# A first-layer chunk moved ahead of the last tile's transposes, and the last transfers shared out anew

## What is computed

```python
e = jnp.stack([tbl_0[ids[:, 0]], ..., tbl_26[ids[:, 26]]], axis=1)      # 27 rows of 128 per sample
interactions = jnp.einsum('bfd,bgd->bfg', e, e)                         # 27 x 27 products per sample
z = jnp.concatenate([bottom, interactions[lower triangle]], axis=1)     # 128 + 351
h = jnp.concatenate([z, bottom], axis=1)                                # 607
h = jnp.maximum(h @ W_top1 + b_top1, 0.0)                               # 607 -> 512
h = jnp.maximum(h @ W_top2 + b_top2, 0.0)                               # 512 -> 256
y = h @ W_top3                                                          # 256 -> 1
```

## Time and profile before

| | |
|---|---|
| median of three runs | 378.94 us (378.78 to 379.65) |
| the profiled execution | 377.31 us |
| its span, first to last instruction | 375.5 us |
| PE busy | 338.1 us (90%) |
| POOL busy | 267.5 us (71%) |
| DVE busy | 247.9 us (66%) |
| ACT busy | 145.9 us (39%) |

### The profile page before, as it was taken

How to read it: one execution, slowest core, us unless ns; L and a number is a source line. 1 busy time by engine, 2 the same in 40 slices (tenths; PEclk the granted TensorE clock), 3 DMA queues, 4 the chain that set the end, 5 groups by cost and what they waited for, 6 DMA issues and landing times.

```text
span 375.5 us, 10311 instructions
## 1 busy us (share of the span) xinstructions
PE 338.1 (90%) x4321; PEld 326.6 (87%) x4321; DVE 247.9 (66%) x332; ACT 145.9 (39%) x280; POOL 267.5 (71%) x292
## 2 busy tenths in 40 slices
PE   0567869998999999999999989998999989997996
PEld 0456759997999999999999989998999989997985
DVE  2699997993699466953698176944598276952051
ACT  1466765615222443155313532145313522155202
POOL 6777777777777777777777777777777777775710
PEclk9998999999999999999999999999999999999999
DMA  7998874336443643345343643355243533323310
GB/s 153 232 223 242 261 209 131 86 81 163 149 121 77 193 114 89 84 100 194 78 108 68 192 108 91 83 136 166 61 111 73 192 107 96 81 60 82 63 16 1
DMA packets 47058, 45.76 MB, mean 122 GB/s; under 512 B 33033, under 2 KB 35930, under 8 KB 47013
## 3 DMA queue, kind: packets, MB, share of 16 engines
q1 hardware_dynamic: 36050, 26.88, 27.3%
q0 software_dynamic: 9184, 17.93, 18.2%
q10 hardware_dynamic: 1779, 0.30, 0.4%
HBM read 39.52 MB, written 5.55 MB: 120 GB/s over the span
## 4 chain that ended last, share of the span: by engine, by line
PE 77%; DMA 7%; DVE 6%; POOL 3%; issue 3%; ACT 3%; SPq 1%
PE work L465 41%; PE gram L492 10%; PE work L477 6%; PE work L518 4%; PE work L519 4%; PE work L520 4%; DMA raw_lo<-in_tbl 4%; DVE onehot L625 3%; DMA emb<-in_tbl,ids_all 3%; POOL emb L433 3%; PE work L535 2%; PE work L537 2%; PE work L536 2%; DVE tab_lo L610 2%; SPq L355 1%
## 5 line engine op out<-in xcount | busy, mean ns | idle before, releaser
L433 POOL DMA_INDIRECT emb<-in_tbl,ids_all x272 | 258.3, 950 | 84.0 <-issue 78.0
L625 DVE TENSOR_TENSOR onehot<-ids_bc,row_idf 125x1024 fp32r<-125x1024 int32 (+2 forms) x232 | 198.8, 920 | 35.7 <-PE work L465 29.4
L465 PE MATMUL work<-onehot,tab_hi 125*128 125x256 f32 x672 | 168.8, 291 | 24.1 <-ACT tab_hi L734 13.7
L465 PE MATMUL work<-onehot,tab_lo 125*128 125x256 f32 x672 | 165.2, 286 | 0.0
L465 PEld LDWEIGHTS work<-onehot,tab_hi 125*128 125x128 f32 x672 | 130.5, 194 | 30.0 <-issue 14.4
L465 PEld LDWEIGHTS work<-onehot,tab_lo 125*128 125x128 f32 x672 | 130.8, 195 | 0.0
L776 ACT COPY embT<-work 128x512 f32<-128x512 f32 (+1 forms) x36 | 26.9, 799 | 103.4 <-PE work L465 103.4
L492 PE MATMUL gram<-embT 128*54 128x52 f32 x1920 | 51.6, 214 | 2.3 <-ACT embT L595 2.1
L492 PEld LDWEIGHTS gram<-embT 128*54 128x54 f32 x1920 | 49.6, 130 | 4.6 <-ACT embT L595 1.3
L477 PE MATMUL work<-ident,emb 128*128 128x128 f32 x272 | 35.4, 275 | 4.7 <-DMA emb<-in_tbl,ids_all 4.7
L783 ACT COPY inter<-gram 118x416 f32<-118x416 f32 x64 | 32.4, 508 | 16.6 <-PE gram L492 14.6
(11 more groups left out here) (55 smaller groups left out, 225.5 us busy)
## 6 DMA issues: line engine op xcount, KB each, us to landing
ids_bc<-in_sel_ids SPq DMA_DIRECT2D x14, 512.0 KB, 4.4
grams<-inter SPq DMA_DIRECT2D x62, 84.5 KB
emb<-in_tbl,ids_all POOLq DMA_INDIRECT x272
ids_bc<-in_sel_ids SPq DMA_DIRECT2D x11, 256.0 KB, 9.5
misc<-in_tbl SPq DMA_DIRECT2D x3, 448.0 KB
inter<-in_tbl SPq DMA_DIRECT2D x3, 448.0 KB
raw_w<-in_W_top SPq DMA_DIRECT2D x4, 256.0 KB, 7.2
misc<-in_bottom SPq DMA_DIRECT2D x8, 128.0 KB
```

The lines of the kernel that those rows point to most:

```text
L433: pool.indirect_dma_start(out=emb[:, t % TILE_SLOTS, f, :], out_offset=None, in_=gather_tables[f], in_offset=bass.IndirectOffsetOnAxis(ap= ...
L465: mm = nc.tensor.matmul(out, part[0:k, CHUNK_AT[f] + c, :], onehot[0:k, at % RING, i * HALF:(i + 1) * HALF], start=(c == 0 and i % 2 == 0 ...
L625: nc.vector.tensor_tensor(onehot[0:k, at % RING, 0:width], ids_bc[0:k, four[0]:four[-1] + 1, :].rearrange("p i n -> p (i n)"), row_idf[0:k ...
```

## The change

It has three parts. First, the bottom chunk of half 6's first layer (12 matmuls) is moved on PE: from behind the products of tile 15 to a place ahead of its transposes. The two banks of that layer are thus claimed earlier, so three banks are left for the five groups of transposes: g3 takes the bank of g0, and g4 that of g1. Second, `take_gram` now notes the banks' uses by selections and transposes alone, since the first layer's two banks are still open when the products start. Third, the 28 packs of the last tile are shared 11, 11, 6 by SP, ACT and POOL, where it was 12, 12, 4.

```diff
-    POOL_PACKS = PACKS[5::6]
+    POOL_PACKS = PACKS[2::5]
     SP_PACKS, ACT_PACKS = [[pack for pack in PACKS if pack not in POOL_PACKS][n::2] for n in range(2)]
...
-    use, fill, used, upto = {}, {}, [0] * BANKS, {}
-
-    def claim(*key):
-        n = use["next"] = use.get("next", -1) + 1
+    use, fill, used, upto, embedded = {}, {}, [0] * BANKS, {}, [0] * BANKS
+
+    def claim(*key, n=None):
+        if n is None:
+            n = use["next"] = use.get("next", -1) + 1
         use[key] = (n % BANKS, used[n % BANKS])
         used[n % BANKS] += 1
+        if key[0] in ("select", "rows"):
+            embedded[n % BANKS] = used[n % BANKS]
...
     def take_gram(t):
-        upto["gram", t] = list(used)
+        upto["gram", t] = list(embedded)
...
-        take_rows(2 * h + 1)
+        if h + 1 == HALVES:
+            claim_mlp1(h - 1)
+            take_rows(2 * h + 1, range(BANKS - 2))
+            first = use["next"] - (BANKS - 3)
+            for g in range(BANKS - 2, NGR):
+                claim("rows", 2 * h + 1, g, n=first + g - (BANKS - 2))
+                signal("rows", 2 * h + 1, g)
+            use["next"] = first + BANKS - 1
+        else:
+            take_rows(2 * h + 1)
         take_gram(2 * h + 1)
         if h < HALVES - 1:
             take_mlp(h - 1, "mlp1")
-    take_mlp(HALVES - 2, "mlp1")
+    signal_mlp1(HALVES - 2)
...
                 mlp3(h - 2)
+                if h == HALVES - 1:
+                    mlp1(h - 1, X_ORDER[:1])
                 rows(2 * h + 1, range(NGR))
                 if h < HALVES - 1:
                     mlp1(h - 1)
                 products(2 * h + 1, range(GRAMS))
 
-            mlp1(HALVES - 2)
+            mlp1(HALVES - 2, X_ORDER[1:])
             mlp1(HALVES - 1, X_ORDER[:1])
```

## The result

The changed kernel took 375.94 us (median of 8 runs, 375.29 to 376.30). Beside it, the kernel before took 378.67 us (8 runs, 377.35 to 379.65). The ratio is 0.9933, with a 95% interval of 0.9914 to 0.9952, so 1.8 to 3.3 us less. I had forecast 377.7 us, in a range of 377.0 to 379.1.

The account below looks back on a forecast made before the run. POOL's gathers, then PE from g4's transposes on, were taken to bound the end. Moving 1.44 us into PE's idle time, less 0.2 for the banks, gains 1.24: 378.94 - 1.24 = 377.7 us, range 377.0 to 379.1.

Parts of the forecast that it names:

- Where PE has room: On PE between transposes of g3 and g4: 1.25 us idle, waiting for g4's gathers, into which the bottom chunk fits.
- The banks' wait: At tile 15's transposes: g3 waits for ACT's copy of g0, g4 for DVE's of g1; g4 starts at 346.0 to 346.15.
- The loss behind it: From g4's transposes on: 0.2 us later, bounds 0 and 0.47, passed into everything behind; products start at 347.8.
- my upper bound: Sum on PE behind the products: at most 1.44 us gained, all twelve moved matmuls without loss; forecast 1.24, lower bound 0.97.
- The packs: Tile 15's packs for half 7: all land in time, tightest by 0.6 us; new shares worth nothing, adding 0.4 us slack.
- The sign I gave: In the changed profile at the end: a rounding released by a DMA would show the prediction wrong.
- The packs didn't set the end: Rival at half 7: packs come just in time and the end moves 0.2 us later, 379.1 us; chance 0.12.
- what the three banks' hand-overs cost: Rival at tile 15's transposes: bank hand-overs of 0.35 us or more cut the gain to 0.5 to 0.97; chance 0.15.
- POOL issued six packs in 4.06 us: Rival at POOL's six packs: GpSimd stands still during DVE's ReLU of half 6, giving 380.5 us; chance 0.06.
- The looser counts: `take_gram` drops a wait for DVE's copy in each half: at most 0.2 us in the whole program, taken as 0.
- The span: Length of the profiled execution: 375.5 us before, less 1.24, gives 374.3.
- The total: Median of runs: 1.63 us above the profiled execution, carried over; 378.94 - 1.24 = 377.7 us.

Follow-up runs that it names:

- the move alone: Against the changed kernel, the bottom chunk still moved but the old pack shares 12, 12, 4 restored: 376.58 us, ratio 0.9946.
- the first set: 30 runs of the unchanged kernel before, on the chip shared by the first four experiments: 378.28 us (377.38 to 380.23).
- the chunk twice: Against the move alone, half 6's bottom chunk runs ahead of the last transposes and once more behind the products, old shares: 378.32 us, ratio 0.999.
- The chunk left out: Against the kernel before, its order and shares kept, half 6's bottom chunk isn't computed at all: 376.50 us, runs in two groups.

## Why the prediction was wrong

- **Where PE has room: right.** The wait for g4's gathers is gone, and the chunk fits there.
- **The banks' wait: right.** ACT ended the copy of g0 at 345.58 (345.04 + 0.54 in the changed trace), forecast 345.57 to 345.67; DVE that of g1 at 345.93, forecast 345.92 to 346.02. ACT began its copy of g4 at 346.74, 0.15 later than 346.59, where I had taken 0.2 for the loss.
- **The loss behind it: mis-sized.** It didn't reach the products. The piece called issue between ACT's copy and the products took 0.20 us instead of 0.35, so they started at 347.60, not 347.8, and the gain on PE was my upper bound, 1.44 instead of 1.24. (From POOL's last gather, 0.07 earlier in the changed profile, it is 1.37.) The shorter hand-over is no accident of one execution: it took 0.35 in all seven profiles with the waits of before, and 0.19 to 0.20 in all five with the chunk moved ahead of the transposes. All five also have the looser counts of `take_gram`, so which of the two shortens it stays open.
- **The packs: right.** All came in time; chunk 0's were ready on DVE 0.6 us before PE wanted them, as forecast. The new shares are worth nothing that can be measured (1.0008 alone). The sign I gave was badly chosen, though: a rounding released by a DMA was to mean that I was wrong, and chunk 0's was, without cost, since DVE asks for it earlier than PE.
- **The rivals: none came.** The packs didn't set the end; what the three banks' hand-overs cost, 0.15 at ACT's copy, didn't reach the products; POOL issued six packs in 4.06 us, in part beside DVE's ReLU.
- **The looser counts** weren't tried alone. I took 0 for them; the products of tile 15 start at 347.60 in both profiles, but the 0.15 of the hand-over may be theirs.
- **The span: right.** 374.1, forecast 374.3. That the two spans can be compared so directly is in part luck: POOL's last gather ended at nearly the same moment in both (343.81 and 343.74), and in the move alone a microsecond later.
- **The total: wrong, and this is the step that failed:** "The median of the runs lies 1.63 above the profiled one; I carry the difference over". I took that difference for an offset that both kernels share. The runs showed that it was not: the profiled execution of before was one in which PE's clock had held, and three of seven profiles with its waits lost 1.4 to 1.6 us to a fall of the clock behind two waits, the first of which the change fills. Of the 30 runs of before ten lie where such a loss would put them, so I take about a third. In the changed kernel no profile shows the fall, and the profiled execution lies at the median. The fall is not the whole of the 1.63: if a third of the executions have it, the median one has none, and the profiled one, at 377.31, was faster than all 30 runs of the first set, with the fall or without: which execution was profiled was chance. Another 0.27 us of the miss came from the median of three runs that I started from (378.94, where the eight have 378.67).

What the filled gap is worth on average can only be estimated, from means of runs, which also carry the differences at POOL's last gather. Before, with a mean of 378.55, against the chunk twice, 378.19: 0.4 us. The chunk left out, 376.80, against the changed kernel, 375.99: 0.8 us. A third of executions at 1.5 us gives 0.5. The moved work is 1.4 by the profiles and 1.7 by the means of the chunk twice (378.19) and the move alone (376.49). Together that is 1.8 to 2.5 us, where the means of before and of the changed kernel lie 2.4 (378.40 and 375.99) and 2.6 us apart (378.49 and 375.93). So the forecast of 1.24 missed a term of about 0.6 us and had 0.2 too little in another; 0.4 to 0.6 us remain that no run explains. A part of them may lie ahead of the change, where POOL's last gather ended at 344.0 in the mean of the five profiles of before and at 343.7 in the two of the changed kernel; that wasn't tested.

The warning stood ahead of the prediction: a profile 1.63 us below the median of runs that spread over 0.9 us was not an execution like them. I should have asked what the others did that this one didn't, and which waits could bring it about.

## What to carry to other kernels

A profile is one execution: where it lies off the median of the runs, ask what the others spent before adding the difference to both sides. A gap on PE can cost more than its length, since the clock may fall behind it, so filling it with work that is due anyway is worth that work and the falls. To compare two profiles of a kernel with scatter from several places, measure from the last event ahead of the change (here the end of POOL's last gather), not from the start of the span.

## What was not expected of the hardware

PE's granted clock fell to the lower of its levels behind two waits of 1.0 to 1.4 us with 0.66 us of transposes between them, in three of seven profiles, and the products that followed took 4.84 to 4.99 us instead of 3.41. With one or both waits filled it didn't fall there in six profiles, and the 50 runs of those kernels show no upper group. The length of the waits doesn't tell the executions apart: the gathers' wait was 1.16 to 1.40 us in the three with the fall and 1.13 to 1.28 in the four without. The Trainium skill, page TensorE: Matmul & The Clock Gate, section HAM oscillation — how this bites in real kernels, describes a kernel whose clock falls again and again because PE waits for DMA between pieces of work. The trace agrees in that the fall comes behind such a wait, with a mean granted clock of 0.57 to 0.64 over 348 to 352 us in the three executions. It differs in that the waits here are shorter than those that the section describes, the second is one for ACT's copy, and the fall comes in some executions only. What decides in which executions it falls stays open.
